# A decoder layer on one core: a moved value sum, a moved output product and a load in two pieces

## The chip, the cores and the metric

The kernel runs on one NeuronCore of a Trainium2 chip. The metric is the device time in microseconds (us) of one launch. Engines are named as in the profile: PE multiplies matrices (PEld is its weight load), DVE is the vector engine, ACT the activation engine, POOL is GpSimd, SP issues DMAs. PS is the accumulator memory (PSUM), in eight banks of 128 x 512 f32.

## What is computed

One decoder layer over 2 x 1024 tokens of width 256: a gated linear recurrence, a cross attention in which each token attends to 64 chosen entries of a context of 64 rows, and a block of causal self attention and 8 experts (top 2, weighted), each followed by a layer norm of the sum.

```python
x = _layernorm(x + _L0_attn_ref(x, ...))            # h = h*exp(g) + k v;  o = (q h) normed, gated, @ Wo
x = _layernorm(x + _L0_xattn_ref(x, ctx, itok, ...))
#   c_sel = c_kv[b, indices];  kv = c_sel @ W_kv_up.T
#   attn = softmax(q . k * SCALE over the 64 entries);  out = (attn @ v) @ W_out.T
x = _layernorm(x + _L0_ffn_ref(x, ...))
#   h = ln(x);  scores = q k / sqrt(16), causal;  a = softmax(scores) v @ Wo + bo + x
#   moe = sum of weighted experts over ln(a);  return moe + a
```

## The kernel before

All instructions are written out by hand, engine by engine, and engines meet in semaphores. The 2048 tokens are four blocks (m = 0 to 3) of four tiles of 128. The program is a row of stages: the recurrence, the cross attention (`cross_blocks`), the self attention (`attend`), the experts. Between stages all engines meet.

**The cross attention.** Since indices choose among 64 context rows, the kernel takes a softmax over the 64 rows with the logarithm of each row's count added. One round is one block m. On PE a round has: `exps(m, 0)` and `exps(m, 1)`, the transposed scores of head pairs 0 to 3 and 4 to 7 less their maxima, which ACT turns into exponentials p0 to p7 (`exps` on ACT, L1210); `c_q` (L1000), the queries of the next block; `values(m, 0)` and `values(m, 1)` (L1128, L1131), the exponentials times the context's values, and their sums, of four pairs each, into banks 6 and 7; `scores(m + 1, t)` (L1085, L1090), the next block's scores for the maxima; `wout` (L122), the output projection; `turn_aug` (L1096), the transposed maxima. DVE divides after each `values` (`divide`, L1290 reciprocal and L1292 multiply), takes the next block's maxima (L1283), then the low part of the transposed maxima (`augTlo`, L1287), which releases `exps(m + 1, 0)`, and between them parts of x and q (`x_parts`, `q_parts`), the residual with its statistics (`residual`) and the layer norm's rows (`normed`, L1301). `values(m, 0)` waits for p3 and for the banks 6 and 7 (for m = 0 until ACT has read the recurrence's last output from them: `self.OA[3]`, "out"), `values(m, 1)` for the first division. `exps(m, 1)` waits for p3.

Ahead of the rounds stand the last two output blocks of the recurrence: `out_product(e, 3, ...)` (L866, L867) makes the last one on PE in banks 6 and 7, four tiles; DVE takes its statistics (`out_stats`), ACT the square root (`out_deviation`, L144), DVE the reciprocal (`out_rstd`), ACT writes the rows (`out_rows`, L886). The weights of the self attention are split once into a high part on ACT (`f_weights_hi`) and a low part on DVE (`f_weights_lo`, L1418). In the last round (m = 3) the projections of the self attention are mixed in.

**The self attention.** Queries and keys go to memory in parts (`qk_parts`) and come back per group of four heads (g = 0 to 7), double buffered in aQ and aK (two buffers each). "Low" keys are tokens 0 to 511 of the sequence, "high" 512 to 1023. A group runs through 36 banks of scores (`scores`, L1833 to L1839) in ten quads; quads 3 to 6 (banks 10 to 25) are low key tiles 0 to 3 against high queries, so bank 21 is the last that reads low key tiles 0 to 2, and bank 25 the last that reads tile 3. Two banks are one of 18 slots of PE's list. Beside them run the units that find the next groups' row maxima (L1770, L1781, L1785). The first unit of group g + 2 stands in slot 15 of group g and needs its low keys. Each load of keys or queries of one half is six DMAs on SP's queue (`load_part`, L1513).

```python
                for g in range(NG - 2):
                    e.wait_ge(SE.sem, SE.at(f"e{LOW_QUERIES}", g))
                    self.load_q(e, g + 2, 0)
                    e.wait_ge(SE.sem, SE.at(f"e{LOW_KEYS}", g))
                    self.load_k(e, g + 2, 0)
                    e.wait_ge(SE.sem, SE.at(f"e{NB_ - 1}", g))
                    self.load_q(e, g + 2, 1)
                    self.load_k(e, g + 2, 1)
```

Of the kernel before, what the change touches and what calls it, by code (L numbers as in the profile page):

```python
# [20 lines left out]
P = 128  # L21
# [5 lines left out]
H = 16  # L27
# [4 lines left out]
BLK = 512  # L32
NB = N // BLK
TB = BLK // P
# [27 lines left out]
class Kernel:  # L62
# [894 lines left out]
    def cross_steps(self):  # L957
# [5 lines left out]
        self.S2 = self.steps("cb_pe2", [f"e{k}" for k in range(H // 2)] + ["pv0", "pv1", "wo"])  # L963
# [54 lines left out]
    def cross_blocks(self, c):  # L1018
# [20 lines left out]
        G2, G3 = (4, 5), (6, 7)  # L1039
        s_cnt, VL, AL, VC, AC = self.c_cnt, self.VL, self.AL, self.VC, self.AC  # L1040
        S1, S2, A1, A2, A3, V1, V2, V3, V4 = self.S1, self.S2, self.A1, self.A2, self.A3, self.V1, self.V2, self.V3, self.V4
# [5 lines left out]
        with nc.Block() as block:  # L1047
# [21 lines left out]
            def _(e):  # L1069
                e.sem_inc(S2.sem, 1)  # L1070
                e.sem_inc(self.FS.sem, 1)
# [46 lines left out]
                def values(m, g):  # L1118
# [14 lines left out]
                    last.then_inc(S2.sem, 1)  # L1133
                def wout(m, ts=range(TB)):
# [3 lines left out]
                    if ts[-1] == TB - 1:  # L1138
                        last.then_inc(S2.sem, 1)
# [11 lines left out]
                self.out_product(e, 3, G3, (0, 1))  # L1151
                e.wait_ge(self.OA[2].sem, self.OA[2].at("out"))
                for m in range(NB - 1):
                    exps(m, 0)
                    if m == 0:
                        self.out_product(e, 3, G3, (2, 3))
                    self.c_q(e, m + 1, 0)
                    exps(m, 1)
                    values(m, 0)
# [35 lines left out]
            def _(e):  # L1195
# [30 lines left out]
                self.out_rows(e, 2, G2)  # L1226
                for m in range(NB - 1):
                    exps(m, range(4))
                    q1(m + 1)
                    if m == 0:  # L1230
                        self.out_deviation(e, 3)
                        self.out_rows(e, 3, G3)
# [3 lines left out]
                    if m == 2:  # L1236
                        self.f_deviation(e, 0)
                        self.f_normed(e, 0)
                    augThi(m + 1)
                    if m + 2 < NB:  # L1240
                        xT1(m + 2)
                    if m == 1:
                        self.f_weights_hi(e)
# [23 lines left out]
            def _(e):  # L1267
# [20 lines left out]
                def divide(m, g):  # L1288
                    e.wait_ge(S2.sem, S2.at(f"pv{g}", m))
# [3 lines left out]
                def residual(m):  # L1293
                    e.wait_ge(S2.sem, S2.at("wo", m))
# [24 lines left out]
                self.out_stats(e, 3, G3)  # L1319
                for m in range(NB - 1):  # L1320
                    q_parts(m + 1)
                    if m == 0:
                        self.out_rstd(e, 3)
# [11 lines left out]
                    if m == 2:  # L1335
                        normed(1)
# [3 lines left out]
                    if m == 1:  # L1340
                        self.f_weights_lo(e)
# [4 lines left out]
                    if m == 1:  # L1346
                        normed(0)
# [159 lines left out]
    def load_part(self, e, dst, slots, n, h, sem):  # L1507
        cols = slice(h * BLK, (h + 1) * BLK)
# [9 lines left out]
    def load_k(self, e, n, h):  # L1518
# [1240 lines left out]
```

## Time and profile before

| what | us |
|---|---|
| median of 3 runs | 1388.56 (1381.78 to 1389.29) |
| the profiled execution, its own time | 1377.45 |
| its span, first to last instruction | 1375.7 |
| busy: PE, DVE, ACT, POOL | 1288.4, 978.7, 647.3, 138.3 |
| stages: to the cross attention, cross attention, self attention, rest | 206.5, 144.5, 281, 744 |

The profile is of one execution. A row of a timeline has the start from the span's start, the duration (of a merged run of instructions), the engine, the line, the operation and what it writes and reads; in square brackets stands how long the engine was idle before it and whose end released it. The granted clock (PEclk) is 1.00 at 2.4 GHz and 0.50 at 1.2 GHz.

### The profile page before, as it was taken

The page shows a single profiled execution, that of the slowest core. Times are in us where ns is not written, and L with a number is a line of the kernel's source. Part 1 is how long each engine was busy: PE and PEld are TensorE (multiplying, and loading weights), DVE is VectorE, ACT ScalarE, POOL GpSimd, SP SyncE. Part 2 cuts the span into 40 slices and gives each one's busy share as a digit, 9 for nine tenths or more (in the row PEclk, how much of TensorE's full clock was granted, in tenths as well). Part 3 has the DMA queues.
Part 4 walks back from the last instruction along what each step waited for, and adds up shares of the span by engine and source line. Part 5 has one row for each costly group of instructions (what it writes and reads, how often), then busy time and mean ns, then how long its engine had stood idle before and what let it go on. Part 6 is the DMA issues. An engine that isn't in the chain of part 4 may idle for free.

```text
span 1375.7 us, 18774 instructions
## 1 busy us (share of the span) xinstructions
PE 1288.4 (94%) x7481; PEld 954.5 (69%) x7481; DVE 978.7 (71%) x1409; ACT 647.3 (47%) x946; POOL 138.3 (10%) x217
## 2 busy tenths in 40 slices
PE   8786868999899999999999999999999999999997
PEld 6354536666655555557788888888888888888886
DVE  7999996798798998756775655655546556555566
ACT  5777664336468887774433423323223223232233
POOL 5000002000514332220000000000000000000000
PEclk9999989999999999999999999999999999999999
DMA  5000001002822212113000012110101102010001
GB/s 139 1 0 1 0 1 35 1 1 81 215 83 57 66 53 55 58 32 108 16 1 16 5 36 68 48 37 31 58 12 47 39 16 69 16 39 16 0 16 46
DMA packets 38599, 55.76 MB, mean 41 GB/s; under 512 B 8976, under 2 KB 23744, under 8 KB 38512
## 3 DMA queue, kind: packets, MB, share of 16 engines
q1 hardware_dynamic: 33328, 43.67, 10.8%
q0 software_dynamic: 3648, 10.09, 2.6%
q8 instruction: 59, 0.97, 0.3%
q10 hardware_dynamic: 1536, 0.81, 0.2%
q14 instruction: 28, 0.23, 0.1%
HBM read 43.73 MB, written 10.55 MB: 39 GB/s over the span
## 4 chain that ended last, share of the span: by engine, by line
PE 51%; DVE 2%; ACT 1%; issue 0%; ACTq 0%; DVEq 0%
PE PS L2460 25%; PE PS L2473 24%; PE PS L122 1%; PE PS L114 0%; PE PS L2486 0%; PE PS L2221 0%; PE PS L2246 0%; DVE OT_all L2616 0%; DVE r_st L2300 0%; DVE r_on L2317 0%; DVE r_on L2297 0%; PE PS L2498 0%; DVE X L2309 0%; DVE x_mid L2607 0%; ACT X L2579 0%
## 5 line engine op out<-in xcount | busy, mean ns | idle before, releaser
L2542 ACT ACTIVATE x_g<-PS,x_bias 128x512 f32<-128x512 f32 x256 | 176.0, 687 | 494.1 <-PE PS L2460 493.7
L2460 PE MATMUL PS<-x_h,x_w 128*128 128x512 f32 x1536 | 399.8, 396 | 0.6 <-ACT x_g L2542 0.6
L2473 PE MATMUL PS<-x_mid,x_w 128*128 128x512 f32 x1488 | 383.9, 393 | 1.2 <-DVE x_w L2212 1.2
L2460 PEld LDWEIGHTS PS<-x_h,x_w 128*128 128x128 f32 x1536 | 286.1, 188 | 66.1 <-ACT x_g L2542 1.5
L2473 PEld LDWEIGHTS PS<-x_mid,x_w 128*128 128x128 f32 x1488 | 279.2, 188 | 65.8 <-DVE x_w L2212 1.7
L2607 DVE CAST x_mid<-x_g 128x512 fp32r<-128x512 f32 x256 | 109.2, 426 | 271.9 <-ACT x_g L2542 271.6
L2081 DVE TENSOR_REDUCE a_M<-PS 128x2 f32<-128x1024 f32 (+1 forms) x144 | 173.0, 1223 | 26.1 <-PE PS L1785 19.8
L2609 DVE TENSOR_TENSOR x_mid<-x_g,x_mid 128x512 fp32r<-128x512 f32 x256 | 177.3, 693 | 8.8
L2021 ACT ACTIVATE f_parts<-PS 128x512 f32<-128x512 f32 x224 | 121.2, 600 | 38.9 <-PE PS L1839 25.6
L1862 PE MATMUL PS<-f_parts,aV 128*32 128x256 f32 (+1 forms) x960 | 75.1, 394 | 0.2 <-POOL f_parts L1676 0.2
L526 DVE TENSOR_TENSOR_SCAN qh<-decay,qh 128x1024 f32<-128x1024 f32 x32 | 73.0, 2280 | 0.0
L696 ACT ACTIVATE c_hot<-c_idxT,c_cid 128x1024 bf16<-128x1024 bf16 x65 | 70.7, 1140 | 3.5 <-PE PS L337 2.2
L2440 POOL DMA_DIRECT2D x_wb<-route_w x31 | 16.8, 540 | 476.5 <-DVE OT_all L2616 453.5
L1839 PE MATMUL PS<-aQ,aK 64*128 64x512 f32 x192 | 50.8, 485 | 1.2 <-ACT f_h L2021 1.2
L1839 PEld LDWEIGHTS PS<-aQ,aK 64*128 64x128 f32 x192 | 20.6, 184 | 38.0 <-ACT f_parts L2021 26.6
L2616 DVE SCALAR_TENSOR_TENSOR OT_all<-PS,x_bias,x_wb 128x512 f32<-128x512 f32 x62 | 46.2, 745 | 0.0
L307 PE MATMUL PS<-vparts,g_sel 128*128 128x512 f32 x128 | 39.9, 437 | 5.8 <-DVE qh L521 4.8
L1676 POOL TENSOR_SCALAR_AFFINE_SELECT f_parts<-f_parts 128x512 f32<-128x512 f32 x45 | 28.7, 637 | 163.3 <-ACT f_parts L2021 143.7
L1781 PE MATMUL PS<-aK,aQ 64*128 64x512 f32 (+3 forms) x256 | 36.4, 330 | 9.1 <-DMA aK<-qk_parts 4.2
L2212 DVE TENSOR_TENSOR x_w<-x_raw,x_w 128x1024 fp32r<-128x1024 f32 x32 | 39.4, 1232 | 1.9 <-ACT x_w L2207 1.9
L521 DVE TENSOR_TENSOR qh<-PS,KT 128x1024 f32<-128x1024 f32 x32 | 38.5, 1205 | 1.3 <-PE PS L314 1.2
L531 DVE TENSOR_TENSOR qh<-qh,QT 128x1024 f32<-128x1024 f32 x32 | 38.8, 1214 | 0.0
(371 smaller groups left out, 1590.5 us busy)
## 6 DMA issues: line engine op xcount, KB each, us to landing
x_raw<-L_ffn_e_w SPq DMA_DIRECT2D x32, 512.0 KB, 3.8
qk_parts<-f_parts SPq DMA_DIRECT2D x16, 512.0 KB, 3.9
x_wb<-route_w POOLq DMA_DIRECT2D x31, 256.0 KB, 3.5
aK<-qk_parts SPq DMA_DIRECT2D x96, 64.0 KB, 2.6
aQ<-qk_parts SPq DMA_DIRECT2D x96, 64.0 KB, 2.5
X<-x SPq DMA_DIRECT2D x4, 512.0 KB, 7.5
out<-X SPq DMA_DIRECT2D x3, 512.0 KB, 2.9
O<-itok_BxSx SPq DMA_DIRECT2D x2, 256.0 KB, 7.8
```

What stands on the lines that cost most here:

```text
L526: e.tensor_tensor_scan(qh[:, jj % RQ, :], decay[:, batch(jj // HD)], qh[:, jj % RQ, :], 0.0, ALU.mult, ALU.add).then_inc(s_h, 1)
L696: e.activation(hot[:, n % RS, :], self.idxT[:, :], ACT.Sign, bias=self.cid[:, c:c + 1], scale=2.0).then_inc(s_sg, 1)
L1839: last = e.matmul(bank, K[q][R, s, tile(TB * h if kind == "k0" else kind)], Q[q][R, s, q0:q0 + BLK], start=True, stop=True)
L1862: last = e.matmul(PS[32 * j:32 * j + 32, 7, dst:dst + w], Vs[m % 2][:, kt, j, :], x, start=k in (0, 3) and half == 0, stop=k in (2, NQD - ...
L2021: e.activation(buf[k][:, j, :], PS[:, 4 + b % 3, :], ACT.Exp).then_inc(A.sem, 1)
L2081: e.tensor_reduce(dst, src, AX.X, ALU.max, negate=True).then_inc(VC.sem, 1)
L2460: last = e.matmul(PS[:, f % 2, :], w1[n % 2][u][:, kt, f * P:(f + 1) * P], self.rows(v, k)[:, kt, :], start=m == 0 and kt == 0, stop=m == ...
L2473: last = e.matmul(PS[:, 2 + 2 * (it % 2) + d, :], w2[n % 2][v][:, f, d * P:(d + 1) * P], mid[u][:, f % RM, :], start=f == 0 and m == 0, st ...
L2542: e.activation(g[s % RG][:, :], PS[:, f % 2, :], ACT.Gelu, bias=b1[:, n, f:f + 1]).then_inc(A.sem, 1)
L2607: e.tensor_copy(mid[0][:, f % RM, :], g[s % RG][:, :]).then_inc(V.sem, 1)
L2609: e.tensor_tensor(mid[1][:, f % RM, :], g[s % RG][:, :], mid[0][:, f % RM, :].bitcast(F32), ALU.subtract).then_inc(V.sem, 1)
L2616: e.scalar_tensor_tensor(out=(y if n else sumT[k])[:, d, :], in0=PS[:, 2 + 2 * (it % 2) + d, :], scalar=b2[:, n, d:d + 1], in1=wb[:, it % ...
```

## The change

In the cross attention `values(m, 0)` moves ahead of `exps(m, 1)` in rounds 0 to 2, and the value sums get a semaphore of their own (S3), since their place among the pairs has changed. The last output of the recurrence (`out_product`, `out_rstd`, `out_deviation` and `out_rows` of block 3) is made whole ahead of round 0. The split of the self attention's weights goes from round 1 to round 0, and the rows of the layer norm (`normed(m - 1)`) go between the maxima and `augTlo`, where they stood already in round 2. In the self attention the load of the low keys of group g + 2 is two loads: tiles 0 to 2 after bank 21 and tile 3 after bank 25, six DMAs each.

```diff
-        self.S2 = self.steps("cb_pe2", [f"e{k}" for k in range(H // 2)] + ["pv0", "pv1", "wo"])
+        self.S2, self.S3 = self.steps("cb_pe2", [f"e{k}" for k in range(H // 2)]), self.steps("cb_pe3", ["pv0", "pv1", "wo"])
...
                 turn_aug(0)
                 turn(1)
-                self.out_product(e, 3, G3, (0, 1))
+                self.out_product(e, 3, G3, range(TB))
                 e.wait_ge(self.OA[2].sem, self.OA[2].at("out"))
                 for m in range(NB - 1):
                     exps(m, 0)
-                    if m == 0:
-                        self.out_product(e, 3, G3, (2, 3))
                     self.c_q(e, m + 1, 0)
+                    values(m, 0)
                     exps(m, 1)
-                    values(m, 0)
                     scores(m + 1, 0)
...
                 self.out_rows(e, 2, G2)
+                self.out_deviation(e, 3)
+                self.out_rows(e, 3, G3)
                 for m in range(NB - 1):
                     exps(m, range(4))
                     q1(m + 1)
-                    if m == 0:
-                        self.out_deviation(e, 3)
-                        self.out_rows(e, 3, G3)
                     exps(m, range(4, NP_))
...
+                    if m == 0:
+                        self.f_weights_hi(e)
                     augThi(m + 1)
                     if m + 2 < NB:
                         xT1(m + 2)
-                    if m == 1:
-                        self.f_weights_hi(e)
...
                 self.out_stats(e, 3, G3)
+                self.out_rstd(e, 3)
                 for m in range(NB - 1):
                     q_parts(m + 1)
-                    if m == 0:
-                        self.out_rstd(e, 3)
...
                     maximum(m + 1, 3)
-                    if m == 2:
-                        normed(1)
+
+                    if m == 0:
+                        self.f_weights_lo(e)
+                    else:
+                        normed(m - 1)
                     augTlo(m + 1)
                     if m + 2 < NB:
                         x_parts(m + 2)
-                    if m == 1:
-                        self.f_weights_lo(e)
...
                     residual(m)
-                    if m == 1:
-                        normed(0)
...
-        LOW_QUERIES, LOW_KEYS = last_bank[2], last_bank[6]
+        LOW_QUERIES, LOW_KEYS = last_bank[2], (last_bank[5], last_bank[6])
...
-                    e.wait_ge(SE.sem, SE.at(f"e{LOW_KEYS}", g))
-                    self.load_k(e, g + 2, 0)
+
+                    e.wait_ge(SE.sem, SE.at(f"e{LOW_KEYS[0]}", g))
+                    self.load_k(e, g + 2, 0, (0, TB - 1))
+                    e.wait_ge(SE.sem, SE.at(f"e{LOW_KEYS[1]}", g))
+                    self.load_k(e, g + 2, 0, (TB - 1, TB))
...
                     if u == 0:
-                        e.wait_ge(s_k[0][m % 2], n)
+                        e.wait_ge(s_k[0][m % 2], n_half * (m // 2 * 2 + 1))
```

PE, round 0, before (L866 and L867 are the recurrence's last output, L1000 `c_q`, L1111 and L1115 `exps`, L1128 and L1131 `values(0, 0)`):

```order
L866 MATMUL PS<-Wo,f_parts 128x256 x2
L867 MATMUL PS<-X,ident 128x256
L1111 MATMUL PS<-vparts,XTp 128x512 x12
...
L866 MATMUL PS<-Wo,f_parts 128x256 x2
L867 MATMUL PS<-X,ident 128x256
L1000 MATMUL PS<-vparts,Wgp 128x512 x12
L1111 MATMUL PS<-vparts,XTp 128x512 x12
...
L1128 MATMUL PS<-pr,c_Vblk 32x512 x4
L1131 MATMUL PS<-pr,c_half 32x512 x4
```

And now:

```order
L866 MATMUL PS<-Wo,f_parts 128x256 x2
L867 MATMUL PS<-X,ident 128x256
L1112 MATMUL PS<-vparts,XTp 128x512 x12
...
L1000 MATMUL PS<-vparts,Wgp 128x512 x12
L1129 MATMUL PS<-pr,c_Vblk 32x512 x4
L1132 MATMUL PS<-pr,c_half 32x512 x4
L1112 MATMUL PS<-vparts,XTp 128x512 x12
```

The output's last two tiles stand ahead of the first pairs, and the value sums ahead of the second pairs, with only `c_q` between them and the exponentials that they need.

DVE, round 1 to the first division of round 2, before (L1287 is `augTlo(2)`, L1418 the weights' low part, L1295 to L139 the residual, L1301 `normed(0)`, L1290 the reciprocal):

```order
L1287 TENSOR_TENSOR augT_lo<-PS,augT_hi 128x512
L987 CAST vparts<-PS 128x512
L992 TENSOR_TENSOR vparts<-PS,vparts 128x512 x2
L1418 SCALAR_TENSOR_TENSOR f_W<-V,f_W 128x512 x3
L1295 TENSOR_TENSOR c_y<-PS,X 128x1024
...
L148 RECIPROCAL c_rstd<-c_sd 128x4
L1301 TENSOR_SCALAR X<-c_y,c_mv,c_rstd 128x256 x4
L1010 TENSOR_SCALAR qT_hi<-PS 128x512
```

And now:

```order
L148 RECIPROCAL c_rstd<-c_sd 128x4
L1299 TENSOR_SCALAR X<-c_y,c_mv,c_rstd 128x256 x4
L1285 TENSOR_TENSOR augT_lo<-PS,augT_hi 128x512
L987 CAST vparts<-PS 128x512
L992 TENSOR_TENSOR vparts<-PS,vparts 128x512 x2
L1293 TENSOR_TENSOR c_y<-PS,X 128x1024
...
L1010 TENSOR_SCALAR qT_hi<-PS 128x512
```

The rows of the layer norm now stand ahead of `augTlo`, and the weights' low part is gone from this round (it stands ahead of round 0's `augTlo`).

SP, the loads of one group of the self attention, before:

```order
L1513 DMA aQ<-qk_parts 16x2x512 x6
L1513 DMA aK<-qk_parts 16x2x512 x6
L1513 DMA aQ<-qk_parts 16x2x512 x6
L1513 DMA aK<-qk_parts 16x2x512 x6
L1513 DMA aQ<-qk_parts 16x2x512 x6
```

And now:

```order
L1509 DMA aQ<-qk_parts 16x2x512 x6
L1509 DMA aK<-qk_parts 16x2x384 x6
L1509 DMA aK<-qk_parts 16x2x128 x6
L1509 DMA aQ<-qk_parts 16x2x512 x6
L1509 DMA aK<-qk_parts 16x2x512 x6
```

The second of these rows was one run of six DMAs and is two, of three quarters and one quarter of the columns.

## Rows read from the trace of the kernel before

**Rows 1.** Cross attention: stretch, its us, busy PE, PEld, DVE, ACT, POOL, clock, DMA.

```profile
206.50:351.00 144.50, 132.72 (x748) 94.84 (x748) 112.89 (x195) 68.47 (x114) 9.83 (x10) 1.00 0.13 43
```


**Rows 2.** Timeline of PE (start, us, line, operation, count, idle before and its releaser).

```profile
228.27 0.97 PE L1111 MATMUL PS<-vparts,XTp 32*128 32x512 f32 x12 [0.60 <-ACT X L886]
...
231.12 1.02 PE L866 MATMUL PS<-Wo,f_parts 128*128 128x256 f32 x4
...
241.36 1.06 PE L1128 MATMUL PS<-pr,c_Vblk 128*32 128x512 f32 x8 [1.82 <-ACT X L886]
...
243.22 0.50 PE L1085 MATMUL PS<-XTp,qT_hi 128*128 128x512 f32 x1
...
247.57 1.06 PE L1128 MATMUL PS<-pr,c_Vblk 128*32 128x512 f32 x8 [0.37 <-DVE c_Kblk L1292]
...
293.40 1.06 PE L1128 MATMUL PS<-pr,c_Vblk 128*32 128x512 f32 x8
```


**Rows 3.** Timeline of ACT in round 0.

```profile
229.93 2.07 ACT L1210 ACTIVATE pr<-PS 128x512 f32<-128x512 f32 x4 [0.41 <-PE PS L1115]
...
239.29 1.93 ACT L886 ACTIVATE X<-PS,go_nmr,go_rstd 128x256 f32<-128x256 f32 x4 [0.44 <-DVE go_nmr L880]
241.24 1.28 ACT L1210 ACT_TABLE_LOAD   x1
```


**Rows 4.** Timeline of DVE in rounds 0 to 2.

```profile
233.90 1.42 DVE L134 BATCH_NORM_STATS2 go_st<-PS 128x6 f32<-128x256 f32 x4 [5.73 <-PE PS L867]
...
243.34 3.36 DVE L1290 RECIPROCAL c_Kblk<-PS 128x512 f32<-128x512 f32 x1 [4.09 <-PE PS L1131]
...
249.61 3.35 DVE L1290 RECIPROCAL c_Kblk<-PS 128x512 f32<-128x512 f32 x1
...
257.69 0.69 DVE L1287 TENSOR_TENSOR augT_lo<-PS,augT_hi 128x512 fp32r<-128x512 f32 x1 [1.75 <-ACT augT_hi L1206]
...
269.31 3.36 DVE L1290 RECIPROCAL c_Kblk<-PS 128x512 f32<-128x512 f32 x1 [2.61 <-PE PS L1131]
...
275.57 3.35 DVE L1290 RECIPROCAL c_Kblk<-PS 128x512 f32<-128x512 f32 x1
...
287.13 1.90 DVE L1418 SCALAR_TENSOR_TENSOR f_W<-V,f_W 128x512 fp32r<-128x512 f32 x3 [0.35 <-ACT f_W L1411]
...
292.23 1.39 DVE L1301 TENSOR_SCALAR X<-c_y,c_mv,c_rstd 128x256 f32<-128x256 f32 x4
...
297.49 3.33 DVE L1290 RECIPROCAL c_Kblk<-PS 128x512 f32<-128x512 f32 x1
```


**Rows 5.** Waits of PE from 430 to 556 us (us in total, times, longest).

```profile
PE PS L1781 <- DMA aK<-qk_parts: 4.0, 5, 1.6
```


**Rows 6.** Timeline of PE at two of those waits.

```profile
523.64 0.50 PE L1781 MATMUL PS<-aK,aQ 64*128 64x512 f32 x2 [1.04 <-DMA aK<-qk_parts]
...
552.31 0.66 PE L1781 MATMUL PS<-aK,aQ 64*128 64x512 f32 x2 [1.55 <-DMA aK<-qk_parts]
```


**Rows 7.** Timeline of SP: runs of six loads each, start and us of issuing.

```profile
435.51 3.29 SPq L1513 DMA_DIRECT2D aK<-qk_parts  x6
...
446.46 4.33 SPq L1513 DMA_DIRECT2D aK<-qk_parts  x6
...
518.16 2.64 SPq L1513 DMA_DIRECT2D aK<-qk_parts  x6
```


**Rows 8.** DMA issues: count, KB each, median us from issue to landing.

```profile
aK<-qk_parts SPq DMA_DIRECT2D x96, 64.0 KB, 2.6
...
route_w<-r_wT POOLq DMA_DIRECT2D x4, 16.0 KB, 1.8
```


**Rows 9.** Busy time in three stretches: a group, the fifth, and within it.

```profile
443.60:471.00 27.40, 26.67 (x290) 15.02 (x290) 24.70 (x24) 22.13 (x41) 10.12 (x13) 1.00 0.22 59
...
526.50:557.40 30.90, 29.02 (x294) 16.72 (x292) 25.58 (x25) 22.47 (x41) 10.79 (x14) 0.92 0.20 52
...
552.70:556.10 3.40, 3.40 (x26) 2.75 (x22) 1.57 (x2) 1.43 (x3) 1.03 (x2) 0.50 0.00 0
```

More of the change, by code:

```diff
@@ L1040, in cross_blocks @@
         s_cnt, VL, AL, VC, AC = self.c_cnt, self.VL, self.AL, self.VC, self.AC
-        S1, S2, A1, A2, A3, V1, V2, V3, V4 = self.S1, self.S2, self.A1, self.A2, self.A3, self.V1, self.V2, self.V3, self.V4
+        S1, S2, S3, A1, A2, A3, V1, V2, V3, V4 = self.S1, self.S2, self.S3, self.A1, self.A2, self.A3, self.V1, self.V2, self.V3, self.V4
         s_banks = lambda t: PS[:, 2 * (t % 2):2 * (t % 2) + 2, :]
@@ L1070, in _ @@
                 e.sem_inc(S2.sem, 1)
+                e.sem_inc(S3.sem, 1)
                 e.sem_inc(self.FS.sem, 1)
@@ L1132, in values @@
                                         pr[:, 4 * g + r, :], start=True, stop=True)
-                    last.then_inc(S2.sem, 1)
+                    last.then_inc(S3.sem, 1)
                 def wout(m, ts=range(TB)):
@@ L1138, in wout @@
                     if ts[-1] == TB - 1:
-                        last.then_inc(S2.sem, 1)
+                        last.then_inc(S3.sem, 1)
                 for m in range(2, NB):
@@ L1288, in divide @@
                 def divide(m, g):
-                    e.wait_ge(S2.sem, S2.at(f"pv{g}", m))
+                    e.wait_ge(S3.sem, S3.at(f"pv{g}", m))
                     e.reciprocal(rs[:, g, :], PS[:, 7, :]).then_inc(V2.sem, 1)
@@ L1293, in residual @@
                 def residual(m):
-                    e.wait_ge(S2.sem, S2.at("wo", m))
+                    e.wait_ge(S3.sem, S3.at("wo", m))
                     e.tensor_tensor(y[m % 2][:, :, :], self.pair_banks(6), X[:, m * TB:(m + 1) * TB, :], ALU.add).then_inc(V3.sem, 1)
@@ L1505, in f_store, with load_part @@
             e.dma_start(dst[n, b, :, :, cols], self.f_part[n][:, :, :].bitcast(F32)).then_inc(self.s_st, 16)
-    def load_part(self, e, dst, slots, n, h, sem):
-        cols = slice(h * BLK, (h + 1) * BLK)
+    def load_part(self, e, dst, slots, n, h, sem, tiles=(0, TB)):
+        cols = slice(h * BLK + tiles[0] * P, h * BLK + tiles[1] * P)
         parts = self.parts.rearrange("q (n s r2 r) t -> q n r2 r s t", s=2, r2=2, r=HD)
@@ L1516, in load_q, with load_k @@
         self.load_part(e, self.Q[n % 2], ((0, 0), (1, 0), (3, 1)), n, h, self.s_q[h][n % 2])
-    def load_k(self, e, n, h):
-        self.load_part(e, self.K[n % 2], ((0, 2), (1, 3), (3, 2)), n, h, self.s_kk[h][n % 2])
+    def load_k(self, e, n, h, tiles=(0, TB)):
+        self.load_part(e, self.K[n % 2], ((0, 2), (1, 3), (3, 2)), n, h, self.s_kk[h][n % 2], tiles)
     def attend_buffers(self, sb):
```

## The prediction

> **What bounds the kernel now.** I read the busy times by stage first. In the cross attention PE is busy for 132.7 of 144.5 us and DVE for 112.9 [rows 1], so neither alone sets the time: the reader should look for the places where one waits for the other. The timelines of PE, ACT and DVE show them, and a round comes out as a loop. `augTlo` releases the first four pairs; PE does first pairs, `c_q`, second pairs, value sums; DVE divides (3.36 us of reciprocal, some 0.7 of multiplying), takes two maxima (some 2.3), divides again, takes two more, and waits 1.75 us for the transposed maxima before the next `augTlo` [rows 4]. While PE works towards `values(m, 0)`, DVE stands idle 4.09 us in round 0 and 2.61 in round 1 [rows 4]; in round 2 it is the other way round: the value sums start at 293.40 [rows 2] and would release DVE at about 295.4, but it divides only at 297.49 [rows 4]. Then I read PE's waits in the self attention: five for low keys, 4.0 us in total, none over 1.6 [rows 5]. All that follows the cross attention starts when that stage and the transfers behind it allow, and its own code is otherwise unchanged, so what the stage gains should reach the end.
>
> **Round 0.** The output's first two tiles end at about 227.7 (0.60 us of idle time ahead of 228.27 [rows 2]). From the start of the other two to DVE's statistics passes 2.78 us (231.12 [rows 2], 233.90 [rows 4]). In one piece they are done at about 230.3, and the first pairs, one exp list of 2.85 us (228.27 to 231.12 [rows 2]), start there, 2.0 us later than now. That looks like a loss but is none: the same two tiles no longer stand behind them. ACT's rows come 5.39 us after the statistics' start now (239.29 against 233.90 [rows 3, 4]), but in that stand the queries' parts on DVE and one of two table loads of 1.28 us. The chain itself is the statistics (1.42 [rows 4]), their aggregation, a root and two small operations; I take 2.8 us, between 1.42 and 5.39, from the row of 1.42 and four short steps. So rows at 233.1, ready at 235.0 (1.93 [rows 3]), table load 1.28, four exponentials 2.07 [rows 3]: `values(0, 0)` starts at 238.4, not 241.36 [rows 2], and PE waits about 2.4 us for it instead of 1.82 [rows 2]. The sums take 1.86 us (241.36 to 243.22 [rows 2]), the second pairs 2.85, so scores start at 243.1, as now (243.22). DVE divides from 240.4 (now 243.34 [rows 4]) and has its first result at 244.5. The scores end near 247.0, `values(0, 1)` doesn't wait (now 0.37 [rows 2]), and the second division starts at 248.9 instead of 249.61 [rows 4]: **-0.7 us**, not the 2.9 by which the first division moved, since PE's list is now the longer way. The weights' low part (1.90) goes into the 1.75 us of idle time ahead of `augTlo` [rows 4]: +0.15. ACT's part of it lies in idle time.
>
> **Round 1.** `augTlo` ends at 258.4 now [rows 4]. From there PE's list is first pairs 2.85, `c_q` 3.0 (of the 11.3 us from 228.27 to the end at 239.5, less two exp lists and two tiles [rows 2]), sums 1.86, second pairs 2.85, two scores 3.8 (243.22 to the end of work ahead of 247.57 [rows 2]), sums 2.0 until DVE starts: with 0.3 us of turning ahead, 16.7. Starting 0.55 earlier it gives 274.5 against 275.57 [rows 4]: **-1.1 us** so far. DVE's own way is shorter: it starts at about 266.7, when the queries' parts are done.
>
> **Round 2.** Here DVE is late for 1.90 us of weights and 1.39 us of rows [rows 4], which both leave the stretch. First pairs start at 284.7 now (293.40 less 2.85, 3.0 and 2.85 [rows 2]), so at 283.6. `c_q` is done at 289.4. Queries' parts and the statistics of block 0 take 3.87 (from 293.62, the end of the rows, to 297.49 [rows 4]): division at 293.3, **-4.2**. PE's list to the second division is sums 1.86, second pairs, two scores and sums 2.0, in all 10.5 from 289.4: 299.9, against 303.8 (297.49 and 4.06 and 2.3): -3.9. I take **-4.0 us** for the stage; the ends are -3 (ACT's chain in round 0 as long as now, or the freed DVE time only partly used) and -5.
>
> **The load in two pieces.** Six issues take 2.64 us when nothing disturbs them, 3.29 in a disturbed run [rows 7], and as many issues are made for the last tile as for all four before. They wait for the same bank 25. So the last piece leaves SP when the whole did, and gains only what a quarter of the bytes lands faster. Bounds: 64 KB land in 2.6 us and 16 KB in 1.8 [rows 8], though those go between other places, so 0.8 us at best and nothing at worst. I take 0.35, the transfer proper without the fixed part. Five waits of 4.0 us in total [rows 5] would lose 1.6 (the shortest is under 0.35). Against it: the first piece starts after bank 21, about 3 us ahead (two slots of some 1.5 us in a group of 27.4 [rows 9]), and takes 2.64, so a disturbed first piece delays the last. When twelve issues come in a row, the second six can take 4.33 [rows 7]. I charge 0.6 us for that: **-1.0 us**, between -4.0 (waits gone) and +4.8 (0.8 us in each of six groups). The 36 added issues lie on SP alone.
>
> The Trainium skill's page "DMA: Bandwidth & Descriptors" (rules for kernel authors, and its fit of a fixed 2.0 us and 436 KB per us) speaks against this part: a transfer under 64 KB is mostly overhead. By it 48 KB less save 0.11 us, the part would be worth 0.5 us before its costs, nothing after them, and the sum -4.0. The landings of 2.6 and 1.8 us [rows 8] agree on the fixed part and leave more for the bytes.
>
> **Sum.** -4.0 - 1.0 = -5.0 us on 1377.45, the profiled execution's own time. That lies 11.1 us under the median of the runs shown, so the timed runs hold losses that this trace doesn't show; on the median of 1388.56 the forecast is **1383.5 us** (-0.36%). A measurement of this kernel tells about 0.5% (6.9 us) from no change, so this reads as no difference.
>
> **The rivals.**
> - **The clock stays up in the self attention (faster).** The longest wait for keys, 1.55 us, is followed by matmuls at 1.2 GHz [rows 6, 9] (0.50 from 552.7 to 556.1); the wait of 1.04 is not. The group took 30.9 us against 27.4 [rows 9]; less the longer wait, the clock cost about 2.4. If the shorter wait keeps 2.4 GHz, the sum is -7.4, 1381.2; if timed runs fall more often, which their 11 us would fit, two more such falls avoided give 1376.4. Against: only one fall in five waits here.
> - **The last piece lands later (near no gain).** Issues behind issues are slow in every group, +2 to +3 us net: 1386.5 to 1387.5.
> - **The clock falls in round 0.** PE's wait of 1.82 there grows to 2.4. At 2.4 us of price: -2.6, 1386. The Trainium skill's page "TensorE: Matmul & The Clock Gate" (the HAM clock gate) says that recent idleness brings 1.2 GHz, which rows 9 bear out; by that rule this rival's price would be paid. The wait of 1.82 kept the clock up.
> - **Slower.** The last piece is over 0.8 us later in every group, so all five waits pass 1.5 us and each drops the clock: +4.0 for waits, four more falls at 2.4, less the stage's 4.0: +9.6, 1398. It decides from the point at which the first piece's issues run into the last's by over 0.8 us each time; only [rows 7]'s 4.33 speaks for it.
>
> **How the numbers follow.** Forecast 0.45; clock stays up 0.27; last piece later 0.13; clock falls in round 0 0.07; slower 0.08. Faster by over 0.5% is the clock case and a tenth from the forecast's edge (-5 in the stage, waits gone): 0.37. Slower 0.08, the rest 0.55. The range goes from 1376, the clock case with two more falls, to 1391, half of the slower case.
>
> **What would show it.** The first division of round 0 at about 240.4 and the second near 249; first pairs of round 1 0.5 us earlier and of round 2 1.1; DVE's division in round 2 released by the statistics and not by the weights; the start of the self attention 4 us earlier. PE's five waits for keys total 2.5 to 3.5 us, each last piece issued at the old place. It is wrong if the stage gains under 3 us (then ACT's chain in round 0 is longer than 2.8, or PE's clock fell), or if the waits vanish or pass 4 us.

## The result and the profile after

The changed kernel's median is 1375.72 us (11 runs, 1372.28 to 1377.27), that of before 1383.53 in the same comparison (11 runs, 1376.07 to 1393.32); the ratio is 0.9945, 95% interval 0.9924 to 0.9966. A second comparison (run 5 below) with more runs of before gave 1376.14 against 1380.40, ratio 0.9966 (0.9949 to 0.9983). The profiled execution took 1372.28 us, 5.17 less than the profiled one of before.

| | before | after |
|---|---|---|
| profiled execution | 1377.45 | 1372.28 |
| span | 1375.7 | 1370.6 |
| cross attention, from PE's first score to the first unit of the self attention | 145.4 (206.60 to 352.00) | 142.7 (205.43 to 348.09) |
| PE's waits for low keys, total, times, longest | 4.0, 5, 1.6 | 1.8, 4, 0.7 |
| busy PE, DVE, ACT, POOL | 1288.4, 978.7, 647.3, 138.3 | 1289.7, 980.1, 644.1, 138.8 |

Busy times by stretch (its us, then busy us of PE, PEld, DVE, ACT, POOL, the granted clock, DMA share and GB/s): the cross attention of the kernel before and of the changed one, each from PE's first score to the first unit of the self attention, and 3 us of the changed kernel's self attention.

```profile
206.60:352.00 145.40, 132.72 (x748) 94.84 (x749) 113.26 (x196) 68.93 (x116) 10.56 (x12) 1.00 0.13 43
```

```profile
205.43:348.09 142.66, 133.27 (x748) 95.88 (x749) 113.84 (x196) 65.94 (x114) 10.39 (x12) 0.99 0.14 44
349.80:353.00 3.20, 3.20 (x9) 2.52 (x8) 1.43 (x2) 0.00 (x0) 3.09 (x4) 0.50 0.57 139
```

[rows 1] cut the stage at rounded times; from its first instruction to its last it takes 142.7 us for 145.4. PE's busy time isn't smaller (133.3 for 132.7), so what went is waiting: PE is idle for 9.4 us of it where it was for 12.7. The clock column is new: 0.99 where before had 1.00. Apart from the last few us of both, the changed kernel's trace has PE at 1.2 GHz near 217, near 350 (last row) and near 578 to 585; the trace of before had it after 206.5 only at 552.7 [rows 9]. So the two traces differ in the change and in where the clock fell.

The timeline of PE after, as [rows 2] (start, us, line, operation, count, idle before and its releaser); 205.43 is the first score, 348.09 the first unit of the self attention:

```profile
205.43 1.60 PE L1086 MATMUL PS<-XTp,vparts 128*128 128x512 f32 x6 [1.31 <-PEq L225]
...
230.56 0.97 PE L1112 MATMUL PS<-vparts,XTp 32*128 32x512 f32 x12
...
238.76 1.06 PE L1129 MATMUL PS<-pr,c_Vblk 128*32 128x512 f32 x8 [2.43 <-ACT pr L1209]
...
247.29 1.06 PE L1129 MATMUL PS<-pr,c_Vblk 128*32 128x512 f32 x8
...
289.28 1.07 PE L1129 MATMUL PS<-pr,c_Vblk 128*32 128x512 f32 x8
...
348.09 0.50 PE L1780 MATMUL PS<-aK,aQ 64*128 64x512 f32 x2 [2.76 <-PEq L1047]
```

The first pairs start at 230.56, at the place forecast (230.3), the value sums of round 0 at 238.76 after a wait of 2.43 (forecast 238.4 and 2.4), and `values(0, 1)` no longer waits. ACT's chain in round 0, as [rows 3]:

```profile
232.66 0.30 ACT L144 ACTIVATE go_sd<-go_mv,eps 128x4 f32<-128x4 f32 x1 [4.06 <-DVE go_mv L139]
233.40 1.93 ACT L886 ACTIVATE X<-PS,go_nmr,go_rstd 128x256 f32<-128x256 f32 x4 [0.45 <-DVE go_nmr L880]
235.35 1.28 ACT L1209 ACT_TABLE_LOAD   x1
236.64 2.06 ACT L1209 ACTIVATE pr<-PS 128x512 f32<-128x512 f32 x4
```

From DVE's statistics at 230.67 (next fence) to ACT's rows at 233.40 pass 2.73 us, for which the forecast took 2.8. One table load stands between the first pairs and the first value sums; in the trace of before there were three between 228 and 243 us (one of them in [rows 3]), and the stage had two more in all. The Trainium skill's page "ScalarE: Activation LUTs" (rules for kernel authors) advises to do all work of one table set before the next; the moved output does that by the way, with 1.28 us for each load here.

The timeline of DVE, as [rows 4]:

```profile
230.67 1.43 DVE L134 BATCH_NORM_STATS2 go_st<-PS 128x6 f32<-128x256 f32 x4 [2.12 <-PE PS L867]
...
240.75 3.36 DVE L1288 RECIPROCAL c_Kblk<-PS 128x512 f32<-128x512 f32 x1 [0.63 <-PE PS L1132]
...
249.29 3.36 DVE L1288 RECIPROCAL c_Kblk<-PS 128x512 f32<-128x512 f32 x1 [0.66 <-PE PS L1132]
...
255.55 1.89 DVE L1414 SCALAR_TENSOR_TENSOR f_W<-V,f_W 128x512 fp32r<-128x512 f32 x3
257.39 0.69 DVE L1285 TENSOR_TENSOR augT_lo<-PS,augT_hi 128x512 fp32r<-128x512 f32 x1
...
266.31 3.35 DVE L1288 RECIPROCAL c_Kblk<-PS 128x512 f32<-128x512 f32 x1
...
274.53 3.36 DVE L1288 RECIPROCAL c_Kblk<-PS 128x512 f32<-128x512 f32 x1 [0.66 <-PE PS L1132]
...
281.00 1.38 DVE L1299 TENSOR_SCALAR X<-c_y,c_mv,c_rstd 128x256 f32<-128x256 f32 x4
282.63 0.69 DVE L1285 TENSOR_TENSOR augT_lo<-PS,augT_hi 128x512 fp32r<-128x512 f32 x1 [0.25 <-ACT augT_hi L1205]
...
293.36 3.32 DVE L1288 RECIPROCAL c_Kblk<-PS 128x512 f32<-128x512 f32 x1
...
299.81 3.36 DVE L1288 RECIPROCAL c_Kblk<-PS 128x512 f32<-128x512 f32 x1
```

The division of round 0 starts at 240.75, the second at 249.29 (forecast 240.4 and 248.9). The weights' low part, 255.55, fills the time ahead of `augTlo` at 257.39, 0.30 earlier than before, where 0.55 was forecast. Round 1's second division starts at 274.53, as forecast (274.5); `normed(0)` at 281.00 is followed by a wait of only 0.25 us for ACT. In round 2 DVE divides at 293.36 (forecast 293.3) and at 299.81 (299.9). The places came out within 0.4 us at each of these. In round 2 the second division has no wait ahead of it, so DVE's own list set it there and not PE's, as the forecast had it; the two end at nearly the same time. The first pairs of round 1 start 0.3 us earlier than before (0.5 forecast), those of round 2 1.0 (1.1), and the self attention 3.9 (4). But all these are positions against the trace of before, and the changed kernel entered the stage 1.2 us earlier, by code that wasn't changed, and then lost 1.7 us (runs 8 and 11 below) to a fall of the clock near 217. Neither stood in the forecast. The two nearly cancel here, and that part of the agreement is luck; the runs below separate them.

Keys, as [rows 5], [rows 8] and [rows 7]: PE's waits in total, times and longest; the last piece's count, KB each and median us to landing; and two runs of issues on SP, which the view merges since they follow each other.

```profile
PE PS L1780 <- DMA aK<-qk_parts: 1.8, 4, 0.7
```

```profile
aK<-qk_parts SPq DMA_DIRECT2D x36, 16.0 KB, 1.7
```

```profile
430.32 6.32 SPq L1509 DMA_DIRECT2D aK<-qk_parts  x12
...
512.61 5.44 SPq L1509 DMA_DIRECT2D aK<-qk_parts  x12
```

Twelve issues take 5.44 us when nothing disturbs them (two times 2.64 and what lies between) and 6.32 in a disturbed group. The last piece lands 1.7 us after its issue, where a whole load took 2.6 [rows 8].

### The profile page after: what moved, and what is told of

It is laid out like the page before. It is cut to its first block, busy times and chain, and to the rows that moved or that the text cites. A ratio compares the mean times of both kernels' runs of the same rounds, so it can differ in the third digit from the quotient of the medians.

```text
span 1370.6 us, 18809 instructions
## 1 busy us (share of the span) xinstructions
PE 1289.7 (94%) x7481; PEld 956.7 (70%) x7481; DVE 980.1 (72%) x1409; ACT 644.1 (47%) x944; POOL 138.8 (10%) x217
## 4 chain that ended last, share of the span: by engine, by line
PE 52%; DVE 2%; ACT 1%; issue 0%; ACTq 0%; DVEq 0%
PE PS L2459 25%; PE PS L2472 24%; PE PS L122 1%; PE PS L114 0%; PE PS L2485 0%; PE PS L2220 0%; PE PS L2245 0%; DVE OT_all L2615 0%; DVE r_st L2299 0%; DVE r_on L2316 0%; DVE r_on L2296 0%; PE PS L2497 0%; DVE X L2308 0%; DVE x_mid L2606 0%; ACT X L2578 0%
```

## The experiments

Medians stand beside the runs of before on the same chip, 1380.88 (29 runs) for the first four, 1380.40 (29) for the second four and 1380.07 (17) for the last. The cuts show the lines that matter. The stage's length is from PE's first score to the first unit of the self attention, from the trace of each run.

**1. The loads alone.** The kernel before with

```diff
-                    e.wait_ge(SE.sem, SE.at(f"e{LOW_KEYS}", g))
-                    self.load_k(e, g + 2, 0)
+                    e.wait_ge(SE.sem, SE.at(f"e{LOW_KEYS[0]}", g))
+                    self.load_k(e, g + 2, 0, (0, TB - 1))
+                    e.wait_ge(SE.sem, SE.at(f"e{LOW_KEYS[1]}", g))
+                    self.load_k(e, g + 2, 0, (TB - 1, TB))
```

> The kernel before with only the low keys' load in two pieces. Theory A (the terms of the forecast hold and the surplus of the timed runs is chance): the five waits of PE for keys sum to 1.8 to 3 us instead of 4.0, median 1 to 2 us below before, scatter of the runs as before. Theory B (shorter waits keep PE's clock at 2.4 GHz in the timed runs, where the kernel before loses it often): the waits are as short, but the median lies 3.5 us or more below before and the runs lie closer together than those of before (17 us from lowest to highest).

Measured: 1379.08 us, ratio 0.9983 (0.996 to 1.0006), so 1.8 us at the medians and not told from nothing. (A twelfth run took 6966 us at a granted clock of 1.00; it isn't in the comparison and why it took so long isn't known.) PE's waits for keys between 400 and 570 us:

```profile
PE PS L1783 <- DMA aK<-qk_parts: 1.0, 3, 0.5
```

They sum to 1.0 us, less than the 1.8 to 3 of both theories. The runs lie between 1374.3 and 1383.1 (standard deviation 3.0 us), those of before between 1374.2 and 1389.0 (4.0). Theory A's median fits, theory B's 3.5 us doesn't. And its trace shows something that the first trace of before doesn't, in the same cross attention code: round 2's wait of PE for the late division is followed by this stretch at 1.2 GHz.

```profile
303.80:307.00 3.20, 3.17 (x16) 0.67 (x16) 2.15 (x2) 0.00 (x0) 0.00 (x0) 0.50 0.00 0
```

**2. The cross attention alone.** The changed kernel with the low keys' load in one run of six after bank 25.

```diff
-                    e.wait_ge(SE.sem, SE.at(f"e{LOW_KEYS[0]}", g))
-                    self.load_k(e, g + 2, 0, (0, TB - 1))
-                    e.wait_ge(SE.sem, SE.at(f"e{LOW_KEYS[1]}", g))
-                    self.load_k(e, g + 2, 0, (TB - 1, TB))
+                    e.wait_ge(SE.sem, SE.at(f"e{LOW_KEYS}", g))
+                    self.load_k(e, g + 2, 0)
```

> The changed kernel with the low keys' load in one run again. Theory A: median 4 to 5 us below before, cross attention's stage 4 us shorter, waits for keys 4 us. Theory B: the same stage gain, median also 4 to 5 us below, but the runs stay as scattered as those of before; the rest to -7.8 belongs to the loads. Theory C (the cross attention alone brings it, since its shorter waits keep the clock there): median 7 us or more below.

Measured: 1376.6 us, ratio 0.9974 (0.9955 to 0.9993), 4.3 us at the medians. The runs lie between 1374.1 and 1380.6, with a standard deviation of 2.0 us where before has 4.0 and run 1 3.0; theory B had this part leave the scatter as it was. PE's waits for keys total 3.2 us. The two ends of the stage on PE:

```profile
208.91 1.62 PE L1086 MATMUL PS<-XTp,vparts 128*128 128x512 f32 x6 [1.31 <-PEq L225]
...
351.56 0.50 PE L1778 MATMUL PS<-aK,aQ 64*128 64x512 f32 x2 [2.73 <-PEq L1047]
```

142.65 us, the changed kernel's length, with one fall of the clock in it too, near 220. Parts 1 and 2 add to 6.1 us at the medians; the changed kernel has 4.3 (run 5), or 5.2 when the first comparison's 11 runs are set against the 29 of before used here. Nothing points to one part needing the other.

**3. The value sums alone.** The kernel before with S3 and

```diff
                     self.c_q(e, m + 1, 0)
+                    values(m, 0)
                     exps(m, 1)
-                    values(m, 0)
```

> The kernel before with only the first value sums ahead of the second four pairs in rounds 0 to 2. All theories: in round 0 the sums still wait for ACT's rows of the recurrence's last output at about 241.4, and now the second pairs wait behind them, so round 0 loses about 2 us; round 1 gains 0.5; round 2 gains 0.2 at most, since DVE is late there for the weights and rows. Stage 0 to +2 us. If it gains 3 us by itself, the moved output, weights and rows were not needed.

Measured: 1384.06 us, ratio 1.0028 (1.0004 to 1.0052), slower. PE's wait in round 0:

```profile
244.22 1.93 PE L1129 MATMUL PS<-pr,c_Vblk 128*32 128x512 f32 x8 [4.77 <-ACT X L886]
```

4.77 us for ACT's rows, with the second pairs now behind it (1.93 us for the eight value sums that took 1.06 in [rows 2], the duration of 1.2 GHz). The stage is 151.1 us long (207.89 to 358.99), 5.7 more than before where 0 to 2 were expected; it holds two falls of the clock, near 219 and behind this wait, which the expectation had not counted. So this move by itself is a loss, and it pays with the other two. No run has the other two without it, so what the value sums' own move adds is not shown.

**4. Both pieces late.** As run 1, with the first piece waiting for bank 25 too.

```diff
-                    e.wait_ge(SE.sem, SE.at(f"e{LOW_KEYS[0]}", g))
+                    e.wait_ge(SE.sem, SE.at(f"e{LOW_KEYS[1]}", g))
```

> As e1, but both pieces wait for bank 25, twelve issues in a row where one list of six stood: the waits for keys grow by the six added issues, 2.6 us each or more, so five or six waits of 3 to 4 us, about +13 to +16 us. Theory B adds falls to 1.2 GHz after such waits, 2.4 us each: six of them give +27 to +30 us in all and the clock reads 0.50 behind each wait. Theory A (falls are chance, not bound to the wait): at most one or two falls, about +15.

Measured: 1415.72 us, ratio 1.0249 (1.0207 to 1.0291), 34.8 us slower, more than either theory's +15 and +27 to +30. PE waits for low keys six times, 17.8 us in total; two of the waits and the clock behind them:

```profile
456.63 0.80 PE L1783 MATMUL PS<-aK,aQ 64*128 64x512 f32 x2 [3.53 <-DMA aK<-qk_parts]
...
521.39 0.50 PE L1783 MATMUL PS<-aK,aQ 64*128 64x512 f32 x2 [2.22 <-DMA aK<-qk_parts]
```

```profile
455.10:465.00 9.90, 8.37 (x54) 5.19 (x54) 4.83 (x4) 4.82 (x8) 3.80 (x5) 0.50 0.13 32
523.40:526.60 3.20, 3.20 (x26) 1.58 (x26) 3.06 (x3) 2.44 (x4) 2.55 (x4) 0.50 0.09 23
```

The waits grew by 13.6 us over the 4.2 that before's trace has in the same six places (its five of [rows 5] and one of 0.23 ahead of them). The rest, some 21 us, goes with the clock, whose mean over the runs is 0.9607 against 0.9789 (before's 29 runs less one that recorded 0.931). All six waits, of 2.2 to 3.6 us, meet a stretch at 0.50. So long waits for keys go with falls, as theory B says. But the length alone doesn't decide: PE waits 2.7 us at the end of the cross attention in the first trace of before, in run 1 and in run 6, and keeps 2.4 GHz there.

**5. The changed kernel again.**

> The changed kernel once more, beside runs of before on the same chip. If the forecast's terms hold (stage -4, loads -1) and the first comparison's -7.8 owed the rest to which runs of before were drawn, the difference of medians is 4.5 to 6 us. If the timed runs really hold more than the trace shows (the clock), it is 7 us or more again. The mean granted clock of each run is read beside its time: at equal clock the changed kernel should lie 4.5 to 5 us under before.

Measured: 1376.14 us against 1380.40, ratio 0.9966 (0.9949 to 0.9983): 4.3 us. That is just under the 4.5 to 6 expected and far from 7. The changed kernel's median is the first comparison's within 0.5 us (1375.72), that of before is 3.1 lower, so the surplus of the first comparison lies with before's runs: by these numbers, their draw. Each run's mean granted clock stands beside its time. At a clock of 0.980, 17 runs of before (of the 75 beside runs 1 to 11) average 1379.8 us and the two of the changed kernel (of 23) 1375.0; at 0.979 it is 1380.8 (3 runs) and 1376.3 (12), at 0.981 1378.8 (9) and 1373.8 (4). At equal clock the difference is 4.6 to 5.0 us in these three.

**6. Weights and rows stay.** The changed kernel with the DVE and ACT order of before for them.

```diff
-                    if m == 0:
-                        self.f_weights_lo(e)
-                    else:
-                        normed(m - 1)
+                    if m == 2:
+                        normed(1)
                     augTlo(m + 1)
                     if m + 2 < NB:
                         x_parts(m + 2)
+                    if m == 1:
+                        self.f_weights_lo(e)
```

(and `normed(0)` behind `residual(1)`, `f_weights_hi` in round 1)

> The changed kernel with the weights' split and the rows of normed(0) back in their old places (after round 1's maxima and residual). My theory: rounds 0 and 1 keep their gain of 1.1 us or a little more, round 2's first division is late for DVE again and the stage loses 2.9 us of its 4; median about 2.5 to 3 us above the changed kernel, and PE waits some 2 us ahead of its second value sums in round 2 as before. Rival: DVE catches up elsewhere, loss under 1 us.

Measured: 1377.72 us, ratio 0.998 (0.9964 to 0.9996), 1.6 us over the changed kernel's median on that chip. In the trace, DVE and PE in round 2:

```profile
287.30 1.90 DVE L1415 SCALAR_TENSOR_TENSOR f_W<-V,f_W 128x512 fp32r<-128x512 f32 x3 [0.34 <-ACT f_W L1408]
...
292.40 1.38 DVE L1299 TENSOR_SCALAR X<-c_y,c_mv,c_rstd 128x256 f32<-128x256 f32 x4
...
297.67 3.33 DVE L1288 RECIPROCAL c_Kblk<-PS 128x512 f32<-128x512 f32 x1
```

```profile
301.86 1.06 PE L1129 MATMUL PS<-pr,c_Vblk 128*32 128x512 f32 x8 [2.12 <-DVE c_Kblk L1290]
```

The division comes at 297.67, behind 1.90 and 1.38 us of the two pieces, and PE waits 2.12 us for its result, as before. The stage is 145.5 us (206.69 to 352.16) with one fall of the clock in it, 2.8 us longer than the changed kernel's 142.7 with one fall: the 2.9 expected. The rival, a loss under 1 us, is out by that; the timed loss of 1.6 is smaller than the 2.5 to 3 us expected but within what such medians tell. The fall lies in round 0, behind PE's wait of 2.47 us for the exponentials:

```profile
238.50:241.70 3.20, 3.20 (x16) 0.42 (x8) 0.89 (x2) 0.25 (x1) 0.00 (x0) 0.50 0.00 0
```

**7. The output stays.** The changed kernel with `out_product`, `out_deviation`, `out_rows` and `out_rstd` of block 3 in the places of before.

```diff
-                self.out_product(e, 3, G3, range(TB))
+                self.out_product(e, 3, G3, (0, 1))
...
                     exps(m, 0)
+                    if m == 0:
+                        self.out_product(e, 3, G3, (2, 3))
                     self.c_q(e, m + 1, 0)
```

> The changed kernel with the recurrence's last output back in its old place: its last two tiles behind the first pairs, its root and rows behind the first exponentials, while the value sums stand ahead of the second pairs. My theory: round 0 is as in the run with the value sums alone, where PE waited 4.77 us for ACT's rows and lost 3 to 4 us (the second pairs stand behind the wait), rounds 1 and 2 gain as in the changed kernel: the stage is about 3.5 us longer than the changed one's, and PE's wait of 4.8 us in round 0 drops the clock where it did there, 1 to 2 us more. Median 3.5 to 5.5 us above the changed kernel.

Measured: 1379.49 us, ratio 0.9998 (0.9983 to 1.0012), 3.35 us over the changed kernel, at the low edge of the 3.5 to 5.5 expected. PE in round 0:

```profile
243.84 1.93 PE L1129 MATMUL PS<-pr,c_Vblk 128*32 128x512 f32 x8 [4.76 <-ACT X L886]
```

The same wait as in run 3 (4.76), followed by the same fall. The stage is 148.2 us (207.54 to 355.73). Against run 3, with falls of the clock at the same two places, it is 2.9 us shorter: that is the worth of the moved weights and rows, which run 6 puts at 2.8. Against the changed kernel's stage it is 5.5 us longer, with the second fall in it.

**8. Rows shared, a try at a better version.** The changed kernel with the lines below; `values(0, 0)` also waits for DVE's two rows.

```diff
                 self.out_rstd(e, 3)
+                V3o = self.OV[3]
+                e.wait_ge(V3o.sem, V3o.at("nmr"))
+                for t in (2, 3):
+                    last = e.tensor_scalar(X[:, 3 * TB + t, :], PS[:, G3[1], t % 2 * D:(t % 2 + 1) * D], self.o_rstd[1][:, t:t + 1],
+                                           self.o_nmr[1][:, t:t + 1], ALU.mult, ALU.add)
+                last.then_inc(V3o.sem, 1)
...
                 self.out_deviation(e, 3)
-                self.out_rows(e, 3, G3)
+                e.activation(self.f_nmr[:, 0:1], self.eps[:, 0:1], ACT.Exp)
+                self.out_rows(e, 3, G3, (0, 1))
```

> An attempt at a better version: the changed kernel with two of the four row tiles of the recurrence's last output written by DVE (idle there for 3.0 us) and ACT's exponential table loaded ahead of its rows, in its wait for them, by one dummy activation. The exponentials of round 0 should start at about 235.3 instead of 236.64, PE's wait of 2.43 us shrink to 1.1, and the whole be 1.2 us faster than the changed kernel, which the timed runs can hardly tell, but the trace can. If PE's wait doesn't shrink, something else than ACT's chain holds the exponentials.

Measured: 1373.74 us (6 runs) against 1380.40, ratio 0.9947 (0.9927 to 0.9967). ACT's chain and PE's wait:

```profile
232.29 0.30 ACT L144 ACTIVATE go_sd<-go_mv,eps 128x4 f32<-128x4 f32 x1 [4.06 <-DVE go_mv L139]
232.60 1.28 ACT L1228 ACT_TABLE_LOAD   x1
233.90 0.20 ACT L1228 ACTIVATE f_nmr<-eps 128x1 f32<-128x1 f32 x1
234.01 1.00 ACT L886 ACTIVATE X<-PS,go_nmr,go_rstd 128x256 f32<-128x256 f32 x2
234.90 2.05 ACT L1210 ACTIVATE pr<-PS 128x512 f32<-128x512 f32 x4
```

```profile
237.01 1.07 PE L1130 MATMUL PS<-pr,c_Vblk 128*32 128x512 f32 x8 [1.06 <-ACT pr L1210]
```

The table load lies in ACT's wait for the row factors, two rows take 1.00 us, the exponentials start at 234.90 (235.3 expected) and PE waits 1.06 us in place of 2.43. How much of that is the shared rows and how much the early table load was not tested apart.

**9 and 10. Two more traces of the kernel before**, unchanged.

> The kernel before, looked at once more: where its clock falls. If its scatter comes from waits in the cross attention and for keys that only sometimes meet a fall, the stretches at 0.50 lie elsewhere than in the first trace (where one followed the 1.55 us wait for keys): behind the waits of 1.82 us in round 0 or 2.12 us in round 2, or behind another wait for keys. If the falls lie at the same places, this isn't the cause.

> The same as the run before it, for a third trace of the kernel before: between the traces the time should go with the number of stretches at 0.50, about 1 us for each 0.001 of the mean granted clock.

Measured: 1380.82 us at a mean clock of 0.978, and 1389.79 at 0.972, beside the first trace's 1377.45 at 0.984. In the ninth run a wait for keys of 1.04 us, and windows after round 2's wait of 2.12 us, after the 2.73 us at the stage's end and after that one (303.00, 353.30 and 444.60):

```profile
442.31 0.50 PE L1781 MATMUL PS<-aK,aQ 64*128 64x512 f32 x2 [1.04 <-DMA aK<-qk_parts]
```

```profile
303.00:306.40 3.40, 3.40 (x23) 1.74 (x24) 3.40 (x3) 0.00 (x0) 0.00 (x0) 1.00 0.00 0
353.30:356.70 3.40, 3.40 (x22) 2.89 (x23) 3.07 (x3) 1.49 (x4) 3.34 (x3) 1.00 0.50 135
444.60:447.80 3.20, 3.20 (x28) 1.73 (x20) 3.17 (x3) 2.64 (x4) 2.88 (x4) 0.50 0.13 42
```

In the tenth, three waits of PE (round 2, the meeting of all engines ahead of the self attention, low keys) and the stretch behind each:

```profile
305.88 1.93 PE L1128 MATMUL PS<-pr,c_Vblk 128*32 128x512 f32 x8 [2.11 <-DVE c_Kblk L1292]
...
357.77 0.80 PE L1781 MATMUL PS<-aK,aQ 64*128 64x512 f32 x2 [2.74 <-PEq L1047]
...
560.18 0.50 PE L1781 MATMUL PS<-aK,aQ 64*128 64x512 f32 x2 [1.14 <-DMA aK<-qk_parts]
```

```profile
305.90:309.10 3.20, 3.20 (x16) 0.62 (x16) 2.09 (x2) 0.00 (x0) 0.00 (x0) 0.50 0.00 0
357.10:363.70 6.60, 5.93 (x22) 4.84 (x23) 3.58 (x3) 2.08 (x4) 6.49 (x7) 0.50 0.41 115
562.00:568.50 6.50, 6.50 (x41) 2.87 (x42) 3.73 (x4) 4.57 (x7) 3.80 (x5) 0.50 0.26 71
```

The same waits of 2.1 us in round 2 and 2.7 us at the stage's end kept 2.4 GHz in the ninth run and lost it in the tenth. Its stage is 148.7 us (209.10 to 357.77) against 145.4 in the other two, with two falls in it, near 220 and at 305.8. A wait for keys of 1.25 us in the tenth run (at 531.93) kept 2.4 GHz, the one of 1.14 lost it. So the scatter of the kernel before goes with the falls, and a wait that brings one in one execution doesn't in the next. Nor are the falls independent: of the five traces with before's cross attention, the three with a fall near 219 (runs 1, 4 and 10) are the three that fell in round 2 as well (stages of 148.7 us each), and the first and the ninth had neither (145.4 each). PE's waits ahead of the two places, up to 1.1 and 2.1 us, are the same in all five; what sets the pair apart is not shown.

**11. Rows shared again.**

> The kernel with shared rows and the early table load once more. If its gain over the changed kernel is real, it lies 6 to 7.5 us under before again (the changed kernel 4.3 and 5.2 on these chips); if the first was chance, 4 to 5.

Measured: 1374.56 us (12 runs) against 1380.07 (17), ratio 0.9959 (0.9942 to 0.9977): 5.5 us, between the two expected bands (6 to 7.5, and 4 to 5) and over the changed kernel's 4.3 and 5.2. In its trace the stage is 141.2 us (206.42 to 347.64) with a fall near 218; the changed kernel's, with a fall at the same place, is 142.7. So the trace shows 1.4 us, and the timed runs are too coarse to tell it from the changed kernel. It has the lowest medians measured.

## Why the prediction was right and wrong

**The forecast was -5.0 us; it measured -5.2 between the two traces, -4.3 in the second comparison, -7.8 in the first.** The measured median of 1375.72 lies just under the range's low end of 1376.0, and 7.8 us under the forecast of 1383.5. That the traces give -5.2 is in part luck: of the spans' 5.1 us, 1.2 lie ahead of the stage, in unchanged code (its start lies anywhere from 205.4 to 209.1 us in the thirteen traces), 2.7 in the stage and 1.2 behind it, with different falls of the clock in both traces.

**What failed is the step "on the median of 1388.56 the forecast is 1383.5 us".** It took the median of three runs for the kernel's level and laid the whole range on it. With 29 runs twice and 17 once, before's median is 1380.1 to 1380.9 on these chips, and only 5 of the 75 runs reach 1388.5 us: the median of three was a bad draw, some 8 us too high. The gain of 5.0 on 1380.5 gives 1375.5. The working also said that the three runs' 11.1 us over the trace meant losses that the trace doesn't show. That was right, as runs 9 and 10 show: the same kernel took 1377, 1381 and 1390 us with a mean clock of 0.984, 0.978 and 0.972. But a typical run loses 3 us against that trace and not 11, and the range should in any case have reached down to the trace's own 1377.45 less 5, which is 1372.4.

**The stage (-4.0): right, and 0.4 too small.** As traced it gained only 2.7 us (145.4 to 142.7), which is under the 3 that the prediction named as its sign of being wrong, and for a reason that it named beside it: PE's clock fell. With a fall near 218 in it, the changed kernel's is 142.7 us (142.6 in run 5), run 11's 141.2; run 8, the same kernel as run 11 without a fall in the stage, has 139.6 (206.75 to 346.31). So that fall costs 1.7 us (before's two falls cost 3.3, 148.7 against 145.4), the changed kernel's stage without it is 141.0 (worked out, not traced), and its gain 4.4. One row was read 0.2 us short: two scores of round 0 take 4.0 us (243.22 to 247.20, [rows 2]) where the working has 3.8 for round 1; in the changed kernel round 1's take 3.8. Round by round the places fitted: the product ahead of the first pairs cost nothing (ACT's chain in round 0 took 2.73 us for 2.8), PE's list and not DVE set the second division in rounds 0 and 1, and round 2 gained the weights and rows, 2.8 us by run 6 and 2.9 by runs 7 and 3.

**The loads (-1.0): the size of the waits was cautious, the sum about right.** Waits for keys (six places) total 4.2, 3.2, 3.6, 3.2 and 2.9 us in the five traces with one load (before, runs 9, 10, 2, 3), and 1.8, 1.0, 2.4, 2.3, 1.2, 1.5 and 2.3 in the seven with two pieces (after, runs 1, 5, 6, 7, 8, 11): 3.4 and 1.8 on average. So 1.6 us of waiting goes, where the forecast had 1.6 before its costs and 1.0 after them, and the 2.5 to 3.5 us of waits that it named as its sign were missed. Both terms were off: the last piece lands some 0.8 us sooner (1.7 or 1.8 us by group, where the six low key loads of before's trace took 2.4 to 2.7) and not 0.35. Part of that has no wait to shorten (two of before's six were under 0.25 us), and part goes to issues that are late in disturbed groups (6.32 us for twelve where 5.44 is undisturbed); how the rest divides was not traced. The timed runs can't tell this part from nothing (run 1). By the rule on small transfers of the Trainium skill's page "DMA: Bandwidth & Descriptors" (rules for kernel authors) the part would have been worth 0.5 at best; the waits show more. The fit on that page is for loads issued by GpSimd, where these are SP's, and its fixed part of 2.0 us is already over the 1.7 and 1.8 us in which 16 KB land here.

**The clock stays up (chance 0.27): not confirmed, and its premise fell.** The forecast read from one trace that a wait of 1.55 us loses the clock and one of 1.04 doesn't. In runs 9 and 10 waits of 1.04 and 1.14 for keys lost it, and round 2's wait of 2.1 kept it in two traces of this code (the first and run 9) and lost it in three (runs 1, 4 and 10). The scatter of the runs (standard deviation) is 4.0 us for before, 3.0 for the loads alone and 2.0 for the cross attention alone on one chip, 2.9 for before and 1.8 for the changed kernel on another. With 11 or 12 runs each, run 1's and run 2's can't be told apart for certain. Why the cross attention's part narrows them was not tested by itself; round 2's wait of 2.12 us, which is gone, is one cause that fits.

**The clock falls in round 0 (0.07): not seen** in the traces of the changed kernel and run 2, whose wait of 2.4 us was followed by 1.00. In run 6 the clock fell behind the same wait (0.50 from 238.5), so it does happen there. The rival put a price of 2.4 us on it; falls in this stage cost 1.7.

**Slower (0.08) and the late last piece (0.13): no.** The waits shrank in every trace with two pieces. Run 4 shows what late pieces cost when they go further than the slower rival's 0.8 us: 34.8 us for six waits of 2.2 to 3.6.

**The chances.** No difference had 0.55. The first ratio's 0.55% lies just outside 0.5%, the second's 0.34% inside; both intervals hold 0.36%, the forecast.

## What to carry to other kernels

Before a forecast is laid on a median, look how far the runs lie apart: where the slowest and fastest differ by more than the expected gain, a few runs are no level, and the trace's own time belongs in the range. When a piece of work is moved ahead on an engine, follow the longest list that releases the next engine: here the first division of round 0 starts 2.6 us earlier than in the trace of before and the second only 0.3, since it now waits for PE's list. And a move can be a loss by itself while the group that holds it is a gain: the value sums alone cost 3 us, since what they wait for was late.

## What the runs showed of the hardware that I hadn't expected

A mean granted clock lower by 0.001 goes with about 1 us on this kernel: 1377.45 at 0.984, 1380.82 at 0.978, 1389.79 at 0.972, all of one program, and 1.05 us by a straight line through 74 runs of before (correlation 0.94; the 75th, at 0.931 and 1382.74 us, lies far off it). A fall in the cross attention costs 1.7 us (139.6 against 141.2 in two traces of one kernel). The same wait brings a fall in one execution and none in another, up to 2.7 us at least (2.73 at the stage's end in run 9, 2.74 in run 10); the six waits of 2.2 to 3.6 us in run 4 all brought one. The Trainium skill's page "TensorE: Matmul & The Clock Gate" (the HAM clock gate) says that the clock follows how busy PE has been recently; these traces agree in so far as the falls stand behind waits of PE (0.50 behind 2.11, 2.74 and 1.14 us in run 10), and show besides that one trace tells little of how often.
